# Counts from a piece's landing, a smaller memset, the last block in two halves, and packing dealt by a table

## The chip, the core and the metric

The kernel runs on one core of one Trainium2 chip. The metric is the device time of one execution, in microseconds; the kernel before takes 1273.65 us (median of three runs). The engines are TensorE (PE, with its weight loads as PEld), VectorE (DVE), ScalarE (ACT), GpSimd (POOL) and SyncE (SP), whose queue issues the large DMAs here.

## The reference

Two graph layers over one dense adjacency matrix of 8192 x 8192, with 64 features a node:

```
x:   (8192, 64) float32        adj: (8192, 8192) float32 of zeros and ones
# layer 0
deg = clip(sum(adj, axis=1) + 1, 1)
z   = concat([x, (adj @ x + x) / deg]) @ W0 + b
y   = layernorm(x + l2_normalize(relu(z)))
# layer 1, two hops
u = y
for k in range(2):
    u = tanh(concat([adj @ u, u], axis=1) @ W1[k])
out = layernorm(y + u)
```

`adj` has 268 MB, so it is read once. The kernel checks that it holds only zeros and ones, packs it to bits in SBUF while the first product runs, and makes the two products of layer 1 from the packed bits.

## The kernel before

**Streaming stage.** `adj` is cut into 8 x 8 blocks of 1024 x 1024. For each block row J the columns come in the order `ORDERS[J]`, each in two pieces, so that a block row has 16 steps and the stage 128 (step n = 16 J + s; the piece of step n is piece n). A piece is 2 MB and comes in two loads of 1 MB (128 x 2048 float32), each in one of four input slots `raw[:, u]`, with u = 0, 1 for even and 2, 3 for odd pieces. A piece passes through these hands:

1. SP issues its loads when the slots are free (L416 to L419).
2. VectorE *marks* each slot: 64 where the value is one, as bytes in `marks` (L905).
3. ScalarE *counts* the nonzero values of each slot in two instructions (L467); after the second, the slot is free (`counted`).
4. TensorE *packs*: 32 small matmuls of `marks` with powers of two (L648), into the PSUM bank `ps_pack`. There is one such bank, so a pack waits for the save of the one before (`pack_saved`).
5. VectorE *saves* the pack as bytes in `packed` (L910), and *expands* it into `planes` by eight operations (L923).
6. TensorE multiplies: 16 matmuls (a light step), or 24 where a column lies in a finished block row (a heavy step), since the first hop of layer 1 is then done as well (L657).

The orders are written out by hand. On TensorE, step n is: pack piece n + 1, multiply piece n, and in the first eight steps of a block weigh one tile of the block row before (L686). On VectorE, step n is: mark the first slot of piece n + 2, drain a weighed tile (L965 to L969), save piece n + 1, expand it, mark the second slot of piece n + 2, and in steps 8 to 14 of a block do parts of the row's norms (`FINISH`, L984 to L1008). Two of these parts need an inverse root from GpSimd (L580 and L582, L587 and L589). `save_acc` on ScalarE (L478) copies the sums of a block out of PSUM between two counts.

At the start GpSimd sets a third of the feature table to zero (L591, 128 x 8192 bfloat16), of which block row 0 reads only the first eight tiles.

**Second stage.** `UNITS` lists 150 units of half a block. Of each, VectorE takes two bits at a time from `packed` (`two_bits`, L1100 or, for both halves, L1115), ScalarE and VectorE widen them to `wide` (L503, L1129), and TensorE multiplies (L826). At the end of a row its sums are copied (L530), weighed with the row's own features (`weigh_own`, L786 and L788), and finished: addition, tanh on ScalarE, addition of `x1_sum` (made on GpSimd, L608), mean, square, variance, root on GpSimd, product, store. The last row does this in two halves after the last unit, with the seven operations of `finish_last` for both halves in turn.

## Time and profile before

| | |
|---|---|
| runs | 1273.53, 1273.65, 1277.28 us |
| profiled execution | 1273.58 us, span 1271.7 us |
| PE busy | 1195.5 us, 94% |
| DVE busy | 988.7 us, 78% |
| ACT busy | 899.5 us, 71% |
| POOL busy | 96.8 us, 8% |
| DMA | 274.64 MB; in the first 60% of the span 309 to 385 GB/s in a slice of a fortieth |

The span is the time from the first to the last instruction of the profiled execution, and the execution's own time is 1.9 us longer. Matmuls overlap by their modelled ends, so that PE's busy time says less than what stands ahead of a wait: where PE is idle, the profile names who ended the wait. The first 780 us or so are the streaming stage and the rest is the second stage.

### The profile page before, as it was taken

What the parts mean: (1) busy time and instruction counts of PE and PEld (TensorE: products, weight loads), DVE (VectorE), ACT (ScalarE), POOL (GpSimd) and SP (SyncE); (2) the same over time, 40 slices, a digit from 0 to 9 for tenths busy, and PEclk for the clock granted to TensorE, in tenths of its full rate; (3) what the DMA queues carried; (4) which work ended last, traced back from release to release, by engine and by line L of the source; (5) the groups of instructions that cost most, each with busy time, mean ns of one, the idle gap of its engine ahead of it and who ended that gap; (6) DMA issues with size and microseconds to landing.
All of it is one profiled execution on the core that took longest, in us unless ns stands there. A gap on an engine that the chain in (4) does not pass through costs nothing.

```text
span 1271.7 us, 25078 instructions
## 1 busy us (share of the span) xinstructions
PE 1195.5 (94%) x9510; PEld 819.7 (64%) x9510; DVE 988.7 (78%) x2641; ACT 899.5 (71%) x1310; POOL 96.8 (8%) x81
## 2 busy tenths in 40 slices
PE   3889989989999999999999999899999999999996
PEld 2445645645655655655655556778888888887775
DVE  7888898798898797798698687876655454778895
ACT  5778878778778678678668565675555555888783
POOL 3000020020020020010020011100000000010211
PEclk9899999999999999999999999899999999999998
DMA  9999999999999999899899880000000000000000
GB/s 322 381 385 370 372 377 364 366 381 356 364 374 375 343 350 379 319 355 361 309 359 346 322 323 4 1 1 1 1 1 1 1 1 1 1 9 9 18 17 19
DMA packets 88042, 274.64 MB, mean 216 GB/s; under 512 B 22384, under 2 KB 22384, under 8 KB 87920
## 3 DMA queue, kind: packets, MB, share of 16 engines
q1 hardware_dynamic: 86880, 272.73, 58.3%
q8 instruction: 79, 1.29, 0.4%
q10 hardware_dynamic: 1040, 0.26, 0.1%
q14 instruction: 43, 0.35, 0.1%
HBM read 270.88 MB, written 2.10 MB: 215 GB/s over the span
## 4 chain that ended last, share of the span: by engine, by line
PE 68%; DVE 15%; DMA 7%; POOL 4%; ACT 3%; issue 3%; DVEq 0%; POOLq 0%; ACTq 0%
PE acc L657 27%; PE acc L826 25%; DMA raw<-in_adj 7%; PE ps_pack L648 6%; DVE marks L905 6%; PE ps_epi L686 3%; ACT raw L467 3%; DVE planes L923 2%; PE ps_pack L788 2%; PE ps_pack L786 2%; POOL root L589 2%; DVE packed L910 1%; POOL root L582 1%; PE ps_epi L766 1%; PE ps_epi L801 1%
## 5 line engine op out<-in xcount | busy, mean ns | idle before, releaser
L467 ACT ACTIVATE raw<-raw 128x1024 f32<-128x1024 uint32 x512 | 535.8, 1048 | 193.2 <-DVE marks L905 192.0
L657 PE MATMUL acc<-planes,feats 128*128 128x512 fp8e4 x2512 | 569.1, 382 | 7.8 <-issue 7.8
L657 PEld LDWEIGHTS acc<-planes,feats 128*128 128x128 bf16 x2512 | 238.7, 98 | 279.6 <-issue 16.6
L905 DVE TENSOR_SCALAR marks<-raw 128x2048 uint8<-128x2048 f32 x256 | 314.4, 1241 | 26.2 <-DMA raw<-in_adj 25.8
L503 ACT ACTIVATE wide<-twos 128x2048 fp32r<-128x2048 fp8e4 x114 | 215.8, 1917 | 111.1 <-PE acc L826 100.8
L1129 DVE TENSOR_SCALAR wide<-twos 128x2048 fp32r<-128x2048 uint8 x114 | 139.4, 1223 | 74.8 <-PE acc L826 74.1
L648 PE MATMUL ps_pack<-pow,marks 128*128 128x64 bf16 x4096 | 141.8, 194 | 44.8 <-DVE marks L905 44.7
L648 PEld LDWEIGHTS ps_pack<-pow,marks 128*128 128x128 fp8e4 x4096 | 135.8, 98 | 67.7 <-issue 58.8
L923 DVE TENSOR_SCALAR planes<-packed 128x128 uint32<-128x128 uint32 x1024 | 150.9, 220 | 23.3 <-DVE packed L910 22.9
L826 PE MATMUL acc<-wide,x_high 128*128 128x512 f32 x512 | 126.7, 394 | 2.5 <-DVE wide L1129 2.2
L910 DVE TENSOR_SCALAR_CACHE_REDUCE packed<-ps_pack 128x512 uint8<-128x512 f32 x128 | 88.0, 687 | 36.8 <-PE ps_pack L648 36.6
L826 PEld LDWEIGHTS acc<-wide,x_high 128*128 128x128 f32 x512 | 96.3, 190 | 25.2 <-DVE wide L1129 4.4
L826 PE MATMUL acc<-wide,y_high 128*128 128x512 f32 x416 | 106.2, 400 | 0.5 <-DVE y_high L1165 0.5
L467 ACT ACTIVATION_READ_ACCUMULATOR raw<-raw 128x1 f32 x512 | 96.3, 188 | 0.0
L826 PEld LDWEIGHTS acc<-wide,y_high 128*128 128x128 f32 x416 | 78.5, 192 | 17.0 <-issue 1.2
L503 ACT ACTIVATE wide<-agg 128x2048 fp32r<-128x2048 fp8e4 x36 | 68.2, 1911 | 20.3 <-PE acc L826 16.3
L1100 DVE TENSOR_SCALAR twos<-packed 128x128 uint32<-128x128 uint32 x312 | 50.1, 224 | 39.0 <-ACT wide L503 37.2
L826 PE MATMUL acc<-wide,x_low 128*128 128x512 f32 x256 | 61.7, 394 | 3.3 <-DVE wide L1129 3.3
L826 PE MATMUL acc<-wide,x_mid 128*128 128x512 f32 x256 | 62.6, 393 | 0.0
L826 PEld LDWEIGHTS acc<-wide,x_low 128*128 128x128 f32 x256 | 47.1, 188 | 15.3 <-DVE wide L1129 5.9
L580 POOL TENSOR_SCALAR stat<-stat 128x8 f32<-128x8 f32 (+1 forms) x9 | 8.7, 969 | 630.7 <-DVE stat L987 630.7
L826 PEld LDWEIGHTS acc<-wide,x_mid 128*128 128x128 f32 x256 | 47.3, 188 | 9.4
(151 smaller groups left out, 960.5 us busy)
## 6 DMA issues: line engine op xcount, KB each, us to landing
raw<-in_adj SPq DMA_DIRECT2D x256, 1024.0 KB, 6.2
zpart<-in_x SPq DMA_DIRECT2D x7, 256.0 KB, 7.7
out<-result SPq DMA_DIRECT2D x7, 256.0 KB, 2.6
zpart<-in_x ACTq DMA_DIRECT2D x1, 256.0 KB, 9.2
out<-result SPq DMA_DIRECT2D x2, 128.0 KB, 2.0
w_own<-in_L_gnn_W SPq DMA_DIRECT2D x8, 16.0 KB, 6.5
w_a<-in_L_gnn_W SPq DMA_DIRECT2D x4, 16.0 KB, 6.6
w_y<-in_L_gnn_W SPq DMA_DIRECT2D x2, 16.0 KB, 6.7
```

The costliest lines, as they stand in the source:

```text
L467: ins = act.activation(words, words.bitcast(U32), ACT.Sign, accum_out=nonzero[:, tile:tile + 1, I])
L503: act.activation(out_ap, twos_of(u).bitcast(F8), ACT.Abs).then_inc(low_ready, 1)
L589: pool.tensor_tensor(root[:, cols], stat[:, cols], minus_half[:, cols], ALU.pow).then_inc(root_ready, 1)
L648: mm = pe.matmul(ps_pack[:, a * NW:(a + 1) * NW], marks[:, h, q, a * P:(a + 1) * P], pow2[:, q, :], start=q == 0, stop=q == QH - 1)
L657: mm = pe.matmul(acc[g][:, h, :], feats[g][:, I * TB + a, :], planes[:, h, a, :], start=(start or g in opens) and a == 0, stop=a == TB - 1 ...
L686: mm = pe.matmul(bank[:, at:at + weights.shape[1]], sums, weights, start=n == 0, stop=n == len(products) - 1, skip_group_check=True)
L826: mm = pe.matmul(acc[acc_of(key)][:, h, :], pair[:, a, :], wide[:, u % AHEAD, a, :], start=begins and a == 0, stop=a == TB - 1, skip_group ...
L905: dve.tensor_scalar(out_ap.bitcast(U8), raw[:, u, :], 1.0, 64.0, ALU.is_equal, ALU.mult).then_inc(marked, 1)
L910: dve.tensor_scalar(bytes_of(J, I, s % 2), ps_pack[:, :], 1.0, None, ALU.mult, ALU.add, accum_out=packsum[:, bass.ds((J * NB + I) * 2 + s ...
L923: ins = dve.tensor_scalar(wide[:, :, bit * NW // 4:(bit + 1) * NW // 4], words, shift, 0x40404040, op, ALU.bitwise_and)
L1100: ins = dve.tensor_scalar(room[:, :, g * NW // 4:(g + 1) * NW // 4], words, 6 - 2 * g, 0xC0C0C0C0, ALU.logical_shift_left, ALU.bitwise_and)
L1129: dve.tensor_scalar(out_ap, twos_of(u), 128.0, 2.0, ALU.is_ge, ALU.mult).then_inc(high_ready, 1)
```

## The change

- **Counts.** ScalarE waits for the landing of a slot and no longer for its mark, and writes its by-product into the free `twos` buffer instead of over the slot. SP waits for count and mark of a slot. `kept_y` moves from `twos` to `agg[0]`, and `save_acc` waits for its readers.
- **Memset.** GpSimd's memset of 8192 columns goes. VectorE sets the 1024 columns that are read, ahead of its first mark.
- **Packing.** `packing_order()` deals the packs to the steps, up to two in a step and up to three pieces ahead. Evaluated, it gives one pack (piece n + 1) to each step up to 22; two to the steps 23, 36, 39, 47 and 53; none to 25, 41, 46, 125, 126 and 127; and one to every other. From step 53 on TensorE packs piece n + 3 in step n.
- **Last block.** The last row's units are ordered by half, so that half 0 closes at unit 145 and half 1 at unit 149. Half 0 is weighed after unit 147, and `finish_last` for half 0 is spread over VectorE's turns from unit 149 on; the last eight units are taken from `packed` one by one.

```diff
-        for col in list(range(1, row + 1)) + [0]:
-            units += halves(row, col, 0, 1)
+        cols = list(range(1, row + 1)) + [0]
+        if row == LAST_ROWS[-1]:
+            units += [(row, col, h, 0, 1) for h in range(2) for col in cols]
+        else:
+            for col in cols:
+                units += halves(row, col, 0, 1)
...
+LOOKAHEAD = 3
+def packing_order():
+    packs, taken, pe, landed, packed_at = [], 0, 0.0, [0.0] * ALL, [0.0] * ALL
+    for n in range(ALL):
+        J, s = divmod(n, STEPS)
+        here = []
+        while taken + 1 < ALL and taken + 1 <= n + LOOKAHEAD and len(here) < 2:
+            p = taken + 1
+            landed[p] = max(landed[p - 1] + STREAM, packed_at[p - 2] + FREED if p > 1 else 0.0)
+            if p > n + 1 and landed[p] + MARKED > pe:
+                break
+            pe = max(pe, landed[p] + MARKED) + PACK
+            packed_at[p] = pe
+            here.append(p)
+            taken = p
+        packs.append(here)
+        heavy = ORDERS[J][s // 2] < J
+        pe += (HEAVY if heavy else LIGHT) + (WEIGH if J > 0 and s < TB else 0.0)
+    return packs
+STREAM, FREED, MARKED, PACK, LIGHT, HEAVY, WEIGH = 5.5, 3.0, 3.0, 1.1, 3.6, 5.3, 1.5
...
-        kept_y = twos[:, 0].rearrange("p a n -> p (a n)").bitcast(F32)
-        sq = agg[0][:, 0:TB * D]
+        signs = twos[:, :, :, :].rearrange("p h a n -> p h (a n)")
+        sq = kept_y = agg[0][:, 0:TB * D]
...
                             sp.wait_ge(counted, 4 * (J * NB + k) + (u - 3))
+                            sp.wait_ge(marked, 4 * (J * NB + k) + (u - 3))
...
-                    act.wait_ge(marked, J * 4 * NB + (4 * k + u + 1))
+                    act.wait_ge(raw_landed[u], J * (16 * NB) + 16 * (k + 1))
+                    slot = 4 * (J * NB + k) + u
+                    if slot > 1:
+                        act.wait_ge(counted, slot - 1)
...
-                        ins = act.activation(words, words.bitcast(U32), ACT.Sign,
+                        ins = act.activation(signs[:, u % 2, q * BLK:(q + 1) * BLK], words.bitcast(U32), ACT.Sign,
...
-            pool.memset(feats[YHI // P][:, :, :], 0.0).then_inc(consts, 1)
...
-                    if J * STEPS + s < ALL - 1:
-                        pack(J, s + 1)
+                    for p in PACKS[J * STEPS + s]:
+                        pack(p // STEPS, p % STEPS)
...
+                    if k == 2 * NB - 1 and LAST_HALF + 2 == u:
+                        weigh_own(k, [0])
...
+                    packs = PACKS[n]
+                    if packs:
+                        mark_next(packs[0], 0)
                     if J > 0 and 1 <= s <= TB:
                         drain(J - 1, s - 1, 1, USES_1 * (J - 1) + 1 + s)
+                    if packs:
+                        save_pack(packs[0])
                     if n + 1 < ALL:
                         dve.wait_ge(pack_saved, n + 2)
+                        nxt = (n + 1) // STEPS
+                        expand(nxt, ORDERS[nxt][(s + 1) % STEPS // 2], (s + 1) % 2, n if n > 0 else None)
+                    if packs:
+                        mark_next(packs[0], 1)
+                    for p in packs[1:]:
+                        mark_next(p, 0)
+                        save_pack(p)
+                        mark_next(p, 1)
...
+            dve.memset(feats[YHI // P][:, 0:TB, :], 0.0).then_inc(lo_zeroed, 1)
...
+                if 0 <= u - FIRST_LAST < 7:
+                    finish_last(u - FIRST_LAST, 0)
             for n in range(7):
-                for half in range(2):
-                    finish_last(n, half)
+                if n > NU + 9 - FIRST_LAST:
+                    finish_last(n, 0)
+                finish_last(n, 1)
```

TensorE at steps 35 to 37 (block 2), in the program before. `ps_pack` rows are packs, `acc` rows the products, `ps_epi` rows the weighing:

```order
L648 MATMUL ps_pack<-pow,marks 128x64 x32
L657 MATMUL acc<-planes,feats 128x512 x16
L686 MATMUL ps_epi<-w_own,featT 128x128
L686 MATMUL ps_epi<-w_y,agg 128x64
L686 MATMUL ps_epi<-w_a,agg 128x64
L686 MATMUL ps_epi<-w_a,agg 128x128
L648 MATMUL ps_pack<-pow,marks 128x64 x32
L657 MATMUL acc<-planes,feats 128x512 x24
```

The same place in the changed program:

```order
L696 MATMUL ps_pack<-pow,marks 128x64 x32
L705 MATMUL acc<-planes,feats 128x512 x16
L734 MATMUL ps_epi<-w_own,featT 128x128
L734 MATMUL ps_epi<-w_y,agg 128x64
L734 MATMUL ps_epi<-w_a,agg 128x64
L734 MATMUL ps_epi<-w_a,agg 128x128
L696 MATMUL ps_pack<-pow,marks 128x64 x64
L705 MATMUL acc<-planes,feats 128x512 x24
```

Two packs of 32 matmuls stand in a row ahead of the products of step 36. VectorE in step 36 before, from the marks ahead of its drain (the second slot of piece 37 and the first of piece 38) on:

```order
L905 TENSOR_SCALAR marks<-raw 128x2048 x2
L965 SCALAR_TENSOR_TENSOR z<-ps_epi,rdeg,bias 128x64
L967 COPY zpart<-ps_epi 128x64
L969 TENSOR_TENSOR z<-z,ps_epi 128x64
L910 TENSOR_SCALAR packed,packsum<-ps_pack 128x512
L923 TENSOR_SCALAR planes<-packed 128x8x16 x8
L905 TENSOR_SCALAR marks<-raw 128x2048 x2
```

And in the changed program:

```order
L955 TENSOR_SCALAR marks<-raw 128x2048 x2
L1023 SCALAR_TENSOR_TENSOR z<-ps_epi,rdeg,bias 128x64
L1025 COPY zpart<-ps_epi 128x64
L1027 TENSOR_TENSOR z<-z,ps_epi 128x64
L968 TENSOR_SCALAR packed,packsum<-ps_pack 128x512
L981 TENSOR_SCALAR planes<-packed 128x8x16 x8
L955 TENSOR_SCALAR marks<-raw 128x2048 x2
L968 TENSOR_SCALAR packed,packsum<-ps_pack 128x512
L955 TENSOR_SCALAR marks<-raw 128x2048 x2
```

A second save with two more marks follows; the second slot of piece 38 is still marked after the expansion, as before. The end of the program on VectorE, from the variance of row 14 (L1244) on, before:

```order
L1244 TENSOR_REDUCE stat<-nonzero 128x8
L1247 TENSOR_TENSOR result<-result,root 128x512
L1264 TENSOR_TENSOR result<-ps_pack,zpart 128x256
L1264 TENSOR_TENSOR result<-ps_epi,zpart 128x256
L1268 TENSOR_TENSOR result<-result,src 128x256 x2
L1271 TENSOR_REDUCE mean<-result 128x4 x2
L1274 SCALAR_TENSOR_TENSOR result<-mean,result 128x256 x2
L1278 TENSOR_TENSOR nonzero<-result 128x256 x2
L1281 TENSOR_REDUCE stat<-nonzero 128x4 x2
L1284 TENSOR_TENSOR result<-result,root 128x256 x2
```

And after (the addition of half 0, L1334, stands two rows ahead of it):

```order
L1334 TENSOR_TENSOR result<-ps_pack,zpart 128x256
L1309 TENSOR_TENSOR nonzero<-result 128x512
L1311 TENSOR_REDUCE stat<-nonzero 128x8
L1338 TENSOR_TENSOR result<-result,src 128x256
L1314 TENSOR_TENSOR result<-result,root 128x512
L1341 TENSOR_REDUCE mean<-result 128x4
L1344 SCALAR_TENSOR_TENSOR result<-mean,result 128x256
L1348 TENSOR_TENSOR nonzero<-result 128x256
L1351 TENSOR_REDUCE stat<-nonzero 128x4
L1354 TENSOR_TENSOR result<-result,root 128x256
L1334 TENSOR_TENSOR result<-ps_epi,zpart 128x256
L1338 TENSOR_TENSOR result<-result,src 128x256
```

All seven operations of half 0 stand ahead of those of half 1, and its second one (L1338) ahead of row 14's last (L1314).

## Rows read from the trace of the kernel before

**Rows 1.** Stretches: blocks 0 to 3, and after the last unit; columns in its head.

```profile
core 0: us, PE busy (x) PEld busy (x) DVE busy (x) ACT busy (x) POOL busy (x), PEclk, DMA share, GB/s
22.30:117.20 94.90, 82.81 (x792) 43.44 (x790) 81.54 (x224) 73.05 (x137) 0.00 (x0) 0.95 1.03 377
117.20:208.50 91.30, 82.86 (x858) 49.56 (x854) 78.57 (x233) 72.51 (x136) 8.20 (x4) 1.00 1.00 369
208.50:299.50 91.00, 85.61 (x875) 51.02 (x871) 78.96 (x233) 72.07 (x136) 8.20 (x4) 1.00 0.99 370
299.50:391.60 92.10, 88.84 (x891) 52.77 (x888) 78.86 (x233) 72.49 (x136) 8.20 (x4) 1.00 0.99 367
...
1256.80:1271.70 14.90, 3.75 (x34) 3.58 (x32) 6.53 (x15) 1.43 (x3) 4.62 (x6) 0.73 0.17 38
```

**Rows 2.** Costliest groups, busy and mean, then idle before; SP's waits.

```profile
L648 PE MATMUL ps_pack<-pow,marks 128*128 128x64 bf16 x4096 | 141.8, 194 | 44.8 <-DVE marks L905 44.7
L923 DVE TENSOR_SCALAR planes<-packed 128x128 uint32<-128x128 uint32 x1024 | 150.9, 220 | 23.3 <-DVE packed L910 22.9
SPq L418 <- ACT raw L467: 638.6, 251, 8.9
```

**Rows 3.** Timeline of the start: start, length, engine, line, instruction, idle before.

```profile
1.24 1.76 DVE L1065 MEMSET feats<- 128x2048 uint32 x1 [1.24 <-PEq L1412]
4.75 6.92 POOL L591 MEMSET feats<- 128x8192 bf16 x1
6.24 7.93 DVE L905 TENSOR_SCALAR marks<-raw 128x2048 uint8<-128x2048 f32 x2 [3.23 <-DMA raw<-in_adj]
12.97 1.06 ACT L467 ACTIVATE raw<-raw 128x1024 f32<-128x1024 uint32 x1 [10.44 <-DVE marks L905]
```

**Rows 4.** Stretches of 2.5 us at the start, columns as rows 1.

```profile
12.50:15.00 2.50, 0.69 (x14) 0.72 (x15) 2.47 (x4) 2.03 (x4) 0.58 (x1) 1.00 1.01 403
15.00:17.50 2.50, 1.17 (x22) 1.01 (x19) 2.40 (x9) 2.24 (x6) 0.00 (x0) 1.00 0.54 141
```

**Rows 5.** Timeline of TensorE, then VectorE, in step 36.

```profile
228.72 1.10 PE L648 MATMUL ps_pack<-pow,marks 128*128 128x64 bf16 x32
229.66 5.34 PE L657 MATMUL acc<-planes,feats 128*128 128x512 fp8e4 x24
...
230.16 0.68 DVE L910 TENSOR_SCALAR_CACHE_REDUCE packed<-ps_pack 128x512 uint8<-128x512 f32 x1
...
231.02 1.18 DVE L923 TENSOR_SCALAR planes<-packed 128x128 uint32<-128x128 uint32 x8 [0.18 <-DVE packed L910]
232.11 1.22 DVE L905 TENSOR_SCALAR marks<-raw 128x2048 uint8<-128x2048 f32 x1
```

**Rows 6.** Timeline of GpSimd's root and the packs in block 2's norms.

```profile
259.01 1.15 POOL L580 TENSOR_SCALAR stat<-stat 128x8 f32<-128x8 f32 x1 [70.00 <-DVE stat L987]
260.24 2.95 POOL L582 TENSOR_TENSOR root<-stat,minus_half 128x8 f32<-128x8 f32 x1
...
263.23 0.69 DVE L990 SCALAR_TENSOR_TENSOR z<-z,root 128x512 f32<-128x512 f32 x1
...
269.02 1.09 PE L648 MATMUL ps_pack<-pow,marks 128*128 128x64 bf16 x32 [1.18 <-DVE marks L905]
...
274.58 1.09 PE L648 MATMUL ps_pack<-pow,marks 128*128 128x64 bf16 x32 [1.01 <-DVE marks L905]
```

**Rows 7.** Timeline of the end, units and last two rows.

```profile
1253.25 3.79 PE L826 MATMUL acc<-wide,x_low 128*128 128x512 f32 x16
...
1255.05 0.69 DVE L1244 TENSOR_REDUCE stat<-nonzero 128x8 f32<-128x512 f32 x1
...
1256.10 1.65 POOL L589 TENSOR_TENSOR root<-stat,minus_half 128x8 f32<-128x8 f32 x1
...
1257.72 1.04 POOL L608 TENSOR_TENSOR src<-y_mid 128x512 f32<-128x512 f32 x1
...
1263.90 0.74 DVE L1281 TENSOR_REDUCE stat<-nonzero 128x4 f32<-128x256 f32 x2
...
1264.69 1.02 POOL L589 TENSOR_TENSOR root<-stat,minus_half 128x4 f32<-128x4 f32 x1
...
1267.35 0.42 DVE L1284 TENSOR_TENSOR result<-result,root 128x256 f32<-128x256 f32 x1 [1.18 <-POOL root L589]
```

More of the change, by code:

```diff
@@ L156 @@
 L2_EPS = 1e-12
+LOOKAHEAD = 3
[18 more added lines that the diff above has]
+STREAM, FREED, MARKED, PACK, LIGHT, HEAVY, WEIGH = 5.5, 3.0, 3.0, 1.1, 3.6, 5.3, 1.5
+PACKS = packing_order()
+TAKEN = [max(sum(PACKS[:n + 1], [0])) for n in range(ALL)]
 def gnn_kernel(nc, x, adj, w0, b0, w1, out):
@@ L375, in gnn_kernel @@
         BITS = 1 + 2 * QH
-        CONSTS = 4
+        CONSTS = 3
         WEIGHTS = 16 * 18
@@ L484, in save_own, with counts_before @@
                 act.activation(featT[:, :], ps_epi[:, :], ACT.Copy).then_inc(epi_drained, 1)
-            for J in range(NB):
-                for s in range(STEPS):
-                    count_step(J, s)
-                    if J > 0 and s < 2:
-                        save_acc(J - 1, s)
-                    if s == STEPS - 1:
+            def counts_before(n):
+                return min(TAKEN[n] + 1, ALL - 1)
+            for p in range(ALL):
+                count_step(p // STEPS, p % STEPS)
+                for J in range(NB):
+                    for h in range(2):
+                        if J < NB - 1 and counts_before((J + 1) * STEPS - 2 + h) == p:
+                            save_acc(J, h)
+                    if counts_before(J * STEPS + STEPS - 2) == p:
                         save_own(J)
@@ L551, in _ @@
                         take_tanh(k)
-            last = result[:, (2 * NB - 1) % 2]
-            for half in range(2):
-                act.wait_ge(own_read, 2 * NB + half)
-                ap = last[:, 4 * half * D:4 * (half + 1) * D]
-                act.activation(ap, ap, ACT.Tanh).then_inc(tanh_done, 1)
+            last_tanh(1)
             with act.If(unless_binary(act) > 0):
@@ L778, in weigh_own @@
                     pe.wait_ge(own_read, k)
-                for half in range(2):
+                for half in part:
                     pe.wait_ge(sums_saved, SAVED[(kind, ROWS[k]), half])
@@ L906, in mark, with mark_next, save_pack @@
                                   ALU.mult).then_inc(marked, 1)
-            def save_pack(J, s, I):
-                dve.wait_ge(pack_done, J * STEPS + (s + 1))
+            def mark_next(p, pair):
+                if p + 1 < ALL:
+                    mark((p + 1) // STEPS, (p + 1) % STEPS, pair)
+            def save_pack(p):
+                J, s = divmod(p, STEPS)
+                I = ORDERS[J][s // 2]
+                dve.wait_ge(pack_done, p + 1)
                 dve.tensor_scalar(bytes_of(J, I, s % 2), ps_pack[:, :], 1.0, None, ALU.mult, ALU.add,
@@ L1087, in two_bits @@
                 row, col, h = UNITS[u][:3]
-                if u >= THIRD:
+                if THIRD <= u and row != LAST_ROWS[-1] or THIRD <= u < LAST_UNITS and row == LAST_ROWS[-1]:
                     if h == 0:
@@ L1316, in _ @@
                             finish_row(k, 5)
-            dve.wait_ge(out_stored[LAST % 2], 16 * ((LAST - NB) // 2))
-            dve.wait_ge(upper_read, NB - 1 - ROWS[LAST])
+                if 0 <= u - FIRST_LAST < 7:
+                    finish_last(u - FIRST_LAST, 0)
             for n in range(7):
-                for half in range(2):
-                    finish_last(n, half)
+                if n > NU + 9 - FIRST_LAST:
+                    finish_last(n, 0)
+                finish_last(n, 1)
             with dve.If(unless_binary(dve) > 0):
```

40 lines of the change are left out of this document (24 added, 16 removed).

## The prediction

> **What bounds the kernel now.** I read the stretches by block first, then who waits for whom, then the timeline at the four places that the edits touch.
>
> The streaming stage is eight blocks of sixteen steps. In the stretches [rows 1] the first four blocks take 94.9, 91.3, 91.0 and 92.1 us. TensorE is idle in them for 12.1, 8.4, 5.4 and 3.3 us (length less busy PE), VectorE is busy for 79 to 82 us, and DMA moves 367 to 377 GB/s with a busy share of 0.99 to 1.03. Three resources are nearly full together, and DMA is the fullest: a step reads 2 x 1.048 MB, which at 370 GB/s is 5.67 us against a measured 5.7. The grouped rows [rows 2] name TensorE's idle time: 44.8 us before the packing matmuls (L648), nearly all ended by VectorE's marks (L905). SP's queue waits 638.6 us for ScalarE's counts, which release the input slots.
>
> TensorE's granted clock is 0.95 in block 0 and 1.00 in the three after it [rows 1]; I take no change of time from it. The profiled execution took 1273.58 us with a span of 1271.7 us, the median of the runs is 1273.65; my sum is made against 1273.6.
>
> **The smaller memset.** A mark takes 1.22 us [rows 5], but the two that start at 6.24 us take 7.93 us together, and ScalarE's first count starts at 12.97 us, released by the first of them. GpSimd's memset (L591) runs from 4.75 for 6.92 us [rows 3], so it ends at 11.67, and 11.67 + 1.22 = 12.89. The first mark stands still behind the memset, for some 5.4 us. The new memset on VectorE is a quarter of the one at 1.24 us that took 1.76 us, about 0.5 us, inside VectorE's 3.23 us of idle time before the first mark: free. If that cover were gone it would cost its 0.5 us.
>
> The Trainium skill, SBUF — State Buffer, § Who interferes with whom, says that VectorE in a two-port mode and GpSimd exclude each other for a whole instruction, whoever started first. By that rule, the trace agrees here: blocked to the memset's end, not slowed in proportion.
>
> Of the 5.4 us less than half arrives. DMA binds block 0, and it lost only what its own gap cost: from 15.0 to 17.5 us it moves 141 GB/s, against 403 in the stretch before [rows 4]. That is (403 - 141) / 403 x 2.5 = 1.6 us, and the refill, with two slots in flight instead of four, starts slowly behind it. **Start: -2.5 us** (bounds -1.6 and -5.4).
>
> **Counts from landing.** Count and mark now run side by side, and a slot comes free at the later of the two, instead of mark 1.2 us + two counts of 1.06 us [rows 3]: some 2.1 us sooner for each slot. Where DMA's queue is already full (share 1.03 and 0.99) this lengthens the queue and not the rate. Taken: 0, since the rows show no faster steady rate; the other end is in the rivals. The added wait on `marked` in SP costs nothing: behind it in SP's queue stand only the next loads, which wait for the same marks anyway.
>
> **The table.** Each of the steps 23, 36, 39, 47 and 53 packs two pieces; 25, 41, 46 and the last three pack none. What two in a row cost is read from step 36 in before [rows 5]. TensorE packs piece 37 from 228.72 and the products follow at 229.66. VectorE saves that pack at 230.16, expands piece 37 at 231.02 for 1.18 us, and then marks the second half of piece 38, 232.11 + 1.22 = 233.33. In before this runs under products of 5.34 us. In the new program, TensorE's second pack stands ahead of those products and VectorE's order is unchanged: save, expand, mark. So the second pack cannot start before 233.35, and TensorE stands idle from 229.7: **3.6 us for each double**. Nothing covers it, because the products are queued behind the pack on the same engine.
>
> Each double also moves one pack of 0.95 us forward (228.72 to 229.66), given back where none is packed.
>
> - Up to block 2: the first double lies in a block where pieces arrive barely in time. It costs 3.6 us, and the free step 25 returns some 2.6 of it, since VectorE and DMA are behind there (my choice between 0 and all of it). -2.5 + 1.0 = **-1.5 us**.
> - Doubles 36, 39, 53: 3 x (3.6 + 0.95) = 13.7. Double 47 lies in the last step of a block, without the drain that stands ahead of the save in the other three: 3.2 + 0.95 = 4.1. Together **+17.8 us**.
> - Step 41 without a pack. Steps 41 to 45 are bound by VectorE, which has marks, a save, an expansion and two operations of the norm to do: packs come 274.58 - 269.02 = 5.56 us apart, and each waits 1.0 us for the marks [rows 6]. Leaving out two marks and a save (2 x 1.22 + 0.68 [rows 5]) shortens VectorE's step by 3.1 us. But its next norm operation (L990, 263.23) needs GpSimd's root, whose two operations start at 259.01 and end at 260.24 + 2.95 = 263.19, 4.2 us in all, just as long as VectorE had marks to make [rows 6]. What the empty step frees is then spent waiting for the root. **+0.2 us** net, bounds -3 and +1.
> - Step 46 without a pack: heavy products (5.34 us) hide what VectorE saves; the pack and the wait before it go: 0.95 + 1.0 = **-2.0 us**.
> - From step 48 on, the wait of 0.18 us between save and expand (22.9 us over 128 steps [rows 2]) is gone, since the piece that is saved is no longer the one expanded. It counts only where VectorE binds, some three steps of a block: 5 x 3 x 0.18 = **-2.7 us**.
> - Last steps: two packs fewer, **-1.9 us**.
>
> Streaming stage: -1.5 + 17.8 + 0.2 - 2.0 - 2.7 - 1.9 = **+9.9 us**.
>
> The same rule of the Trainium skill (SBUF — State Buffer, § Who interferes with whom) would make GpSimd faster in step 41, where no mark of 1.2 us holds the pair: the root took 1.65 us in the tail [rows 7] and 2.95 us beside marks [rows 6]. The stage would then be 1 us shorter, +8.9 us. No row of the trace shows a root beside an empty step.
>
> **The last block in two halves.** The intent is that half 0 is finished under half 1's products. VectorE's order says otherwise. Half 0's seven operations stand ahead of all of half 1's, and its second one needs x1_sum, which GpSimd makes only after row 14's root. In before [rows 7]: reduction at 1255.05, root at 1256.10 for 1.65 us, x1_sum at 1257.72 for 1.04 us. In the new order that reduction comes after half 0's first addition, which waits for its weighing: the last two units start at 1253.25 in before, the weighing takes their place for half of 3.75 us [rows 1], and 1253.25 + 1.9 + 0.42 + 0.7 for the operation between is 1256.3, 1.2 us later. So x1_sum is ready at 1258.76 + 1.2 = 1259.95. Then, at 0.42 us an operation, 0.7 for a whole row, and GpSimd's root done 1.45 us after the reduction (1264.27 to 1265.71): addition 1260.4, row 14's product 1261.1, four operations 1262.8, root 1264.3, product 1264.7. Only now comes half 1: addition, tanh, addition 1.4 us, four operations 1.7, root 1.45, product 0.45: 1269.7. In before the last product ends at 1267.35 + 0.42 = 1267.77. **Tail: +2.0 us**, bounds -3.1 (half 0 out of the way: 0.9 of weighing, 1.0 of VectorE's shared steps, 1.2 of GpSimd's first root) and +3. The last eight units are unpacked one by one instead of in pairs, four more groups of four operations, 4 x 4 x 0.22 (the mean of L923 [rows 2]) = 3.5 us on VectorE over eight units of 1.9 us, of which it fills 1.22 each; no cost taken, and 1 us if a unit waits for it.
>
> **Sum.** 1273.6 + 9.9 + 2.0 = 1285.5 us.
>
> **The rivals.**
> A, faster: DMA has more in it. 403 GB/s stands in [rows 4]; with slots freed 2.1 us sooner, pieces come faster, and the stock of packed ones fills TensorE's idle time of blocks 1 to 3. Three quarters of 8.4 + 5.4 + 3.3 us is -12.8; start -2.5, doubles 47 and 53 in heavy steps +6.8, tail +2.0: 1267.1 us. Against it: a queue full at 1.03 still moves only 377 GB/s. The Trainium skill, HBM Reference, § Specifications (TRN2), states about 425 GB/s for a core that streams alone; by it a piece would take 4.9 us and DMA would bind no block, which is this rival. No block's row shows more than 377.
> B, no change: the doubles stall as I say, but VectorE runs ahead during each stall, and the steps that it binds afterwards (5.4 us in block 2, 3.3 in block 3) lose their idle time. 9.9 - 8.7 + 2.0: 1276.8 us. Against it: the root.
> C, slower still: being two pieces further ahead takes 2 x 5.67 = 11.3 us more of a full queue by step 53. Where marks of the second piece wait for a landing, half of that comes on top: 1291.1 us. It decides if VectorE's marks wait over 5 us longer for DMA than before.
> That the doubles are none (the second piece marked in time) is excluded by VectorE's order; what is left of it is in A.
>
> **Chances.** Forecast 0.53, A 0.17, B 0.18, C 0.12. A measurement here can tell 0.3%, 3.8 us, from no change. Faster is A, 0.17; same is B, 0.18; slower is the forecast and C, 0.65. The forecast's own range is 1281 to 1290 us. The range that should hold 8 in 10 is 1268 to 1292 us: it takes in B and the near half of A, and C beyond its price.
>
> **What would show it.** In the changed profile: the first mark in 1.2 us; the wait of L648's successor for marks up by some 14 us, the five longest after the start about 3.5 us; VectorE's idle time before L990's successor for GpSimd's root grown in blocks 1 and 2; the eight blocks' stretch ending some 10 us later; half 1's addition after half 0's product in the tail. I am wrong if the block lengths 2 and 3 do not grow, if DMA's rate in blocks 1 to 3 exceeds 385 GB/s, or if the tail after the last unit is under 14 us.

## The result, and the profile after

| | before | after |
|---|---|---|
| median of four runs | 1273.59 us | 1290.62 us |
| range | 1271.69 to 1277.28 | 1290.53 to 1293.98 |
| profiled execution, span | 1271.7 us | 1288.7 us |
| mean granted clock | 0.989 | 0.982 |

The ratio is 1.0136, 95% interval 1.0116 to 1.0155: slower, 5 us beyond the 1285.5 us that were predicted. It lies 0.6 us over the forecast's own range of 1281 to 1290 us and inside the one of 1268 to 1292 us. By stages: from the first instruction to the last product of the streaming stage 782.7 us became 797.2 (+14.5, predicted +9.9), and the rest went from 489.1 to 491.5 us (+2.5, predicted +2.0).

The stretches of blocks 0 to 3 and of the end in the profile after, to be held against [rows 1]:

```profile
19.00:115.30 96.30, 80.54 (x793) 42.54 (x791) 81.99 (x225) 72.09 (x134) 0.00 (x0) 0.98 1.03 379
115.30:206.80 91.50, 83.66 (x857) 50.43 (x853) 78.65 (x233) 72.72 (x136) 6.12 (x4) 0.98 0.97 369
206.80:313.90 107.10, 92.54 (x908) 54.86 (x905) 81.34 (x237) 77.07 (x144) 5.86 (x4) 0.94 0.90 340
313.90:410.60 96.70, 92.30 (x923) 55.10 (x919) 80.82 (x237) 77.12 (x144) 8.06 (x4) 0.96 0.96 364
1273.80:1288.70 14.90, 2.23 (x18) 1.86 (x16) 5.92 (x14) 1.01 (x2) 3.87 (x6) 0.68 0.17 38
```

Blocks 2 and 3, which hold the doubles 36, 39, 47 and 53, took 16.1 and 4.6 us more. DMA did not speed up there. It fell to 340 GB/s, and the granted clock fell from 1.00 to 0.94 and 0.96, in stretches in which TensorE is busy for over 85% of the time.

The grouped rows of after (L696 packs, L955 marks, L968 saves, L981 expands, L519 is `save_acc`), against [rows 2]:

```profile
L955 DVE TENSOR_SCALAR marks<-raw 128x2048 uint8<-128x2048 f32 x256 | 308.4, 1219 | 32.1 <-DMA raw<-in_adj 31.9
L981 DVE TENSOR_SCALAR planes<-packed 128x128 uint32<-128x128 uint32 x1024 | 150.1, 220 | 11.7 <-DVE packed L968 6.2 <-PE acc L705 5.4
L696 PE MATMUL ps_pack<-pow,marks 128*128 128x64 bf16 x4096 | 144.6, 195 | 50.3 <-DVE marks L955 50.3
L519 ACT ACTIVATE agg<-acc 128x512 f32<-128x512 f32 x48 | 25.2, 598 | 49.6 <-PE acc L705 49.6
```

TensorE waits 50.3 us for marks (44.7 before), 5.6 us more where the prediction looked for some 14. The sum alone hides the change: the start gave 3 us back, other steps 8.5, and five new waits of 3.1 to 3.9 us, 17.1 us together, came in. The wait between save and expand fell from 22.9 to 6.2 us. ScalarE waits 49.6 us before `save_acc`, where it waited 5.4 before. That is not the table's doing: with the counts alone it already waits 46.0 us, as shown below.

**The table, as the chip ran it.** TensorE, VectorE and ScalarE at the double of step 47:

```profile
290.32 1.22 DVE L955 TENSOR_SCALAR marks<-raw 128x2048 uint8<-128x2048 f32 x1
291.46 0.42 DVE L1090 CAST feats<-agg 128x512 bf16<-128x512 f32 x1
291.91 0.69 DVE L1092 TENSOR_TENSOR feats<-agg,feats 128x512 bf16<-128x512 f32 x1
292.52 1.17 DVE L981 TENSOR_SCALAR planes<-packed 128x128 uint32<-128x128 uint32 x8
292.70 7.03 PE L705 MATMUL acc<-planes,feats 128*128 128x512 fp8e4 x24 [2.40 <-DVE feats L1092]
293.61 1.22 DVE L955 TENSOR_SCALAR marks<-raw 128x2048 uint8<-128x2048 f32 x1
299.57 1.10 PE L696 MATMUL ps_pack<-pow,marks 128*128 128x64 bf16 x32
299.77 1.57 ACT L519 ACTIVATE agg<-acc 128x512 f32<-128x512 f32 x3 [11.40 <-PE acc L705]
300.70 0.69 DVE L968 TENSOR_SCALAR_CACHE_REDUCE packed<-ps_pack 128x512 uint8<-128x512 f32 x1 [5.88 <-PE ps_pack L696]
...
301.58 1.18 DVE L981 TENSOR_SCALAR planes<-packed 128x128 uint32<-128x128 uint32 x8 [0.18 <-DVE packed L968]
...
302.67 2.35 DVE L955 TENSOR_SCALAR marks<-raw 128x2048 uint8<-128x2048 f32 x2
...
304.04 1.87 PE L696 MATMUL ps_pack<-pow,marks 128*128 128x64 bf16 x32 [3.37 <-DVE marks L955]
...
305.71 7.40 PE L705 MATMUL acc<-planes,feats 128*128 128x512 fp8e4 x24
```

The order is the predicted one: pack, save, expand, mark, and only then the second pack, 3.37 us after the end of the first. Two things were not foreseen. The pack after the pause takes 1.87 us instead of 1.10, and the products 7.40 us instead of 5.34. And step 46, which packs nothing, starts its products no earlier, since they wait 2.40 us for VectorE's `feats` (L1092, the features of the finished row).

**The end.** The timeline of after, against [rows 7]:

```profile
1270.47 0.42 DVE L1334 TENSOR_TENSOR result<-ps_pack,zpart 128x256 f32<-128x256 f32 x1 [0.98 <-PE ps_pack L836]
...
1272.59 1.65 POOL L638 TENSOR_TENSOR root<-stat,minus_half 128x8 f32<-128x8 f32 x1
...
1274.20 1.04 POOL L656 TENSOR_TENSOR src<-y_mid 128x512 f32<-128x512 f32 x1
...
1275.28 0.42 DVE L1338 TENSOR_TENSOR result<-result,src 128x256 f32<-128x256 f32 x1 [3.06 <-POOL src L656]
...
1276.43 0.39 PE L836 MATMUL ps_epi<-w_x_pair,agg 128*128 128x64 f32 x2
...
1279.43 0.43 DVE L1354 TENSOR_TENSOR result<-result,root 128x256 f32<-128x256 f32 x1 [1.42 <-POOL root L638]
1279.77 0.42 DVE L1334 TENSOR_TENSOR result<-ps_epi,zpart 128x256 f32<-128x256 f32 x1
```

Half 0 waits 3.06 us for `x1_sum`, and half 1, whose weighing ends at 1276.82, is added at 1279.77, behind half 0's root and product.

### The profile page after: what moved, and what is told of

Read it like the earlier page. It is cut to its first block, busy times and chain, and to the rows that moved or that the text cites. A ratio compares the mean times of both kernels' runs of the same rounds, so it can differ in the third digit from the quotient of the medians.

```text
span 1288.7 us, 25605 instructions
## 1 busy us (share of the span) xinstructions
PE 1202.3 (93%) x9510; PEld 824.1 (64%) x9510; DVE 977.8 (76%) x2658; ACT 903.2 (70%) x1310; POOL 82.9 (6%) x80
## 4 chain that ended last, share of the span: by engine, by line
PE 72%; DVE 9%; DMA 8%; issue 4%; ACT 3%; POOL 2%; SPq 0%; DVEq 0%; POOLq 0%; ACTq 0%
PE acc L705 31%; PE acc L874 25%; DMA raw<-in_adj 8%; PE ps_pack L696 7%; PE ps_epi L734 3%; DVE marks L955 3%; ACT twos L506 2%; PE ps_pack L836 2%; PE ps_pack L834 2%; DVE planes L981 2%; POOL root L638 1%; PE ps_epi L814 1%; PE ps_epi L849 1%; DVE packed L968 1%; DVE wide L1196 1%
## 5 line engine op out<-in xcount | busy, mean ns | idle before, releaser
L506 ACT ACTIVATE twos<-raw 128x1024 uint8<-128x1024 uint32 x512 | 536.1, 1052 | 145.9 <-DMA raw<-in_adj 145.9
L705 PE MATMUL acc<-planes,feats 128*128 128x512 fp8e4 x2512 | 573.2, 384 | 10.2 <-issue 7.8
L955 DVE TENSOR_SCALAR marks<-raw 128x2048 uint8<-128x2048 f32 x256 | 308.4, 1219 | 32.1 <-DMA raw<-in_adj 31.9
L696 PE MATMUL ps_pack<-pow,marks 128*128 128x64 bf16 x4096 | 144.6, 195 | 50.3 <-DVE marks L955 50.3
L696 PEld LDWEIGHTS ps_pack<-pow,marks 128*128 128x128 fp8e4 x4096 | 139.0, 99 | 70.8 <-issue 61.6
L981 DVE TENSOR_SCALAR planes<-packed 128x128 uint32<-128x128 uint32 x1024 | 150.1, 220 | 11.7 <-DVE packed L968 6.2
L968 DVE TENSOR_SCALAR_CACHE_REDUCE packed<-ps_pack 128x512 uint8<-128x512 f32 x128 | 88.0, 688 | 53.6 <-PE ps_pack L696 53.3
L506 ACT ACTIVATION_READ_ACCUMULATOR twos<-raw 128x1 f32 x512 | 97.7, 191 | 0.0
L874 PEld LDWEIGHTS acc<-wide,y_high 128*128 128x128 f32 x416 | 78.9, 193 | 17.4 <-issue 1.5
L519 ACT ACTIVATE agg<-acc 128x512 f32<-128x512 f32 x48 | 25.2, 598 | 49.6 <-PE acc L705 49.6
L874 PEld LDWEIGHTS acc<-wide,x_low 128*128 128x128 f32 x256 | 47.1, 188 | 15.3 <-DVE wide L1196 5.9
L1023 DVE SCALAR_TENSOR_TENSOR z<-ps_epi,rdeg,bias 128x64 f32<-128x64 f32 x60 | 16.7, 282 | 48.6 <-PE ps_epi L734 48.5
```

Of the source, the lines that this page charges most:

```text
L506: ins = act.activation(signs[:, u % 2, q * BLK:(q + 1) * BLK], words.bitcast(U32), ACT.Sign, accum_out=nonzero[:, tile:tile + 1, I])
L696: mm = pe.matmul(ps_pack[:, a * NW:(a + 1) * NW], marks[:, h, q, a * P:(a + 1) * P], pow2[:, q, :], start=q == 0, stop=q == QH - 1)
L705: mm = pe.matmul(acc[g][:, h, :], feats[g][:, I * TB + a, :], planes[:, h, a, :], start=(start or g in opens) and a == 0, stop=a == TB - 1 ...
L874: mm = pe.matmul(acc[acc_of(key)][:, h, :], pair[:, a, :], wide[:, u % AHEAD, a, :], start=begins and a == 0, stop=a == TB - 1, skip_group ...
L955: dve.tensor_scalar(out_ap.bitcast(U8), raw[:, u, :], 1.0, 64.0, ALU.is_equal, ALU.mult).then_inc(marked, 1)
L968: dve.tensor_scalar(bytes_of(J, I, s % 2), ps_pack[:, :], 1.0, None, ALU.mult, ALU.add, accum_out=packsum[:, bass.ds((J * NB + I) * 2 + s ...
```

## The experiments

Twelve kernels ran. Times are medians; "before" stands for its runs beside them (1275.0 to 1275.7 us). The ratio to before carries the comparison. "Step n starts" is the start of its first product (L657 in before) in the trace of the kernel. Kernels with the same first steps differ by up to 1.7 us at step 16, so differences between two kernels below that say nothing there; differences from step to step within a block repeat to some 0.1 us.

### Which parts cost and which give

**one_ahead** is after without its table:

```diff
-PACKS = packing_order()
+PACKS = [[n + 1] if n + 1 < ALL else [] for n in range(ALL)]
```

> The changed kernel with one pack per step again (piece n + 1 in step n, none in the last), all else as changed. Theory (the doubled packs hold TensorE still, and its clock falls behind the pauses): the 14.5 us of the streaming stage go, and the stage ends about 3 us earlier than in the kernel before; with the 2.5 us that the second stage and the end keep, 1272.5 to 1274.5 us. Rival (counts from landing, or ScalarE's reordered copies, cost the time in blocks 2 and 3): the stage stays longer than before, 1280 us or more.

Measured: 1269.3 us, 0.9954 [0.9934, 0.9975]. The table costs 21 us, and the rest is a gain, larger than either theory had.

**memset_alone** is before with the smaller memset (the diff's lines on `feats[YHI // P]`, `consts` and `lo_zeroed`).

> The kernel before with only the smaller memset on VectorE. Theory: the first mark takes 1.2 us instead of 6.7, DMA's gap at 15 us closes in part, and the stage ends 1.5 to 3 us earlier: 1270.5 to 1272 us. Rival (DMA binds block 0 and the gap comes from the counts behind the marks, so that the start is hidden): 1273.5 us, no change.

Measured: 1272.2 us, 0.9974 [0.9960, 0.9988]. Step 0 starts 3.2 us earlier and step 16 1.9 us.

**counts_alone** is before with the diff's lines on `counted`, `marked`, `signs` and `kept_y`.

> The kernel before with only the counts from a slot's landing. Theory (DMA's queue is full, freeing slots sooner only lengthens it): block 1 and 2 lose under 1 us, the wait of ScalarE in block 3 (0.8 us) goes, 1272 to 1274 us. Rival (DMA has more in it once it is fed sooner): blocks 1 to 3 shorter by 3 us each, 1266 us or less, with DMA over 380 GB/s in them.

Measured: 1267.3 us, 0.9937 [0.9914, 0.9960]. Step 0 starts as before, step 8 2.2 us earlier, step 28 5.7 and step 51 6.5. This is the gain that I had put at 0. It lies in blocks 0 and 1 for the most part, and not in each of the first blocks as the rival had it. The block 1 stretch of this kernel, then its marks (L911) and its `save_acc` (L484):

```profile
117.00:208.50 91.50, 86.03 (x902) 52.22 (x901) 82.32 (x243) 76.37 (x142) 8.21 (x4) 1.00 0.99 381
```

```profile
L911 DVE TENSOR_SCALAR marks<-raw 128x2048 uint8<-128x2048 f32 x256 | 313.9, 1244 | 13.6 <-DMA raw<-in_adj 13.2
L484 ACT ACTIVATE agg<-acc 128x512 f32<-128x512 f32 x48 | 25.2, 597 | 46.0 <-PE acc L663 42.1 <-DVE y_high L1022 3.8
```

DMA moved 381 GB/s where it moved 369, at the same busy share of 0.99 and 1.00, and the marks' wait for data halved (25.8 before). That wait is no measure of the gain, though: in counts_memset, which is next, it is 23.2 us for the same gain. ScalarE, no longer held by the marks, now comes early to `save_acc` at each block's end and waits there for the last product.

**counts_memset** has both, and is after without table and halves.

> The kernel before with the counts from landing and the smaller memset: the changed kernel without its table and without the last block in two halves. Theory: the gains add up to 3 us or slightly more, 1269.5 to 1271.5 us, and the difference from the run with the halves (one pack per step) is the price of the halves, 2 to 3 us. Rival (the halves gain 3 us at the end as intended): this run is slower than that one.

Measured: 1266.7 us, 0.9925 [0.9898, 0.9952]. The memset adds nothing to the counts by the end of the stage (-6.6 us against -6.7). one_ahead, which has the halves as well, takes 2.6 us more by the medians, their price as expected.

**late_slots** asks whether the counts give their 6.7 us because slots come free sooner. It is counts_alone with a later release:

```diff
-sp.wait_ge(counted, 4 * (J * NB + k) + (u - 3))
+sp.wait_ge(counted, 4 * (J * NB + k) + (u - 3) + 1)
```

> The kernel before with the counts from landing alone (1267.3 us, 0.9937 of before), with one edit: SyncE issues a load into a slot of raw only when the count of the next slot is done as well, which is about 2.5 us later, where the kernel before issued it. If the 6.7 us that these counts gave come from the slots that are free 2.2 us earlier, and so from loads that start and land earlier, they go with this edit: 1273 to 1277 us, and the marks wait for the data as long as in the kernel before (25 us or more). Rival: they come from ScalarE and VectorE, whose order no longer ties each count to a mark: 1266 to 1269 us, with marks that wait about 13 us for the data.

Measured: 1287.2 us, 1.0096 [1.0062, 1.0131], in runs spread from 1277 to 1301 us. The gain is gone and more with it. The same two rows of this kernel:

```profile
117.00:208.50 91.50, 83.48 (x858) 49.80 (x856) 79.09 (x234) 73.62 (x137) 8.19 (x4) 1.00 0.96 370
```

```profile
L911 DVE TENSOR_SCALAR marks<-raw 128x2048 uint8<-128x2048 f32 x256 | 315.7, 1241 | 52.7 <-DMA raw<-in_adj 49.9 <-PE ps_pack L654 2.4
```

The rival (it is ScalarE's and VectorE's order) falls, since that order is the same here. The edit overshot, and the time is 10 us above my expectation: the starts stay within 2.5 us of before up to step 40, where counts_alone is 5.7 us ahead, and most of the rest is lost just behind block edges (steps 50, 66, 98 and 114), where ScalarE's `save_acc` stands ahead of a count that the release now needs. That it is this order was not tried by itself. So the run shows that the gain hangs on the release of the slots; it does not measure its size.

### What a double costs, and what a lead gives

The base is counts_memset. A table of its own deals the packs:

```diff
+def dealt(doubles, skips):
+    packs, taken = [], 0
+    for n in range(ALL):
+        count = 2 if n in doubles else 0 if n in skips else 1
+        here = list(range(taken + 1, min(taken + count, ALL - 1) + 1))
...
+PACKS = dealt((36,), ())
```

**double36**: step 36 packs two, and packing stays one piece further ahead.

> The base is the kernel with the counts from landing and the smaller memset alone (1266.7 us, 0.9925 of before): no halves, one piece packed in each step. The one change: step 36 packs two pieces, and from there on packing stays one piece further ahead. Prediction's theory: TensorE stands for the second piece's marks, which VectorE does only behind the save and the expansion: the products of step 36 come 3.6 us later, and with the clock that falls after the pause about 4.2 to 6; little of it comes back, so 1270.5 to 1272.5 us. Rival: the further lead lets more be moved or saves later waits, and the whole comes back by the end of the streaming stage: 1266.5 to 1267.5.

Measured: 1268.7 us, 0.9942 [0.9920, 0.9963].

**double36_free41**: `dealt((36,), (41,))`.

> As the kernel with step 36 doubled, and step 41 packs nothing, so that the lead is given back there. If the pack that is left out comes off TensorE's path, step 41's products come 2.4 to 3.4 us earlier than with the double alone, and the sum is 1268 to 1269 us. By the prediction's step (GpSimd's root ends last there, and eats the pack that is gone) nothing comes back: 1270.5 to 1272.5.

Measured: 1272.7 us, 0.9982 [0.9967, 0.9997].

**double36_free46**: `dealt((36,), (46,))`.

> As the kernel with step 36 doubled, and step 46 packs nothing. The prediction had 2.0 us come back there: 1268.5 to 1270.5. The trace of the changed kernel says that step 46's products wait for a part of x1 that VectorE writes later than they could start, so that nothing comes back: within 0.5 us of the kernel with the double alone, and the step's products start no earlier.

Measured: 1273.1 us, 0.9987 [0.9974, 1.0001].

The starts of steps, in us behind the same steps of counts_memset (after in the last column):

```
step   double36   free41   free46    after
 35     +0.13     -0.16    +0.26     +3.86
 36     +5.84     +5.44    +5.57     +9.60
 37     +7.32     +7.27    +6.18    +10.15
 41     +7.24     +6.25    +6.10    +13.34
 43     +6.51     +4.92    +5.38    +11.74
 46     +5.72     +4.91    +4.58    +10.94
 54     +5.79     +4.91    +4.58    +26.77
 70     +4.58     +4.89    +4.56    +25.56
110     +2.01     +4.86    +4.52    +22.98
127     +1.08     +4.86    +4.52    +21.11
```

One double costs 6 to 7.4 us. A lead that is kept gives it back bit by bit: 5.3 us from step 37 to step 110, in the steps of every block in which VectorE's work is the longest, and 0.9 us in step 126, which has nothing left to pack. So for double36 the price was over the first theory's 4.2 to 6 us, and the rival had the return. A lead that is given up in step 41 returns 2.4 us by step 43 and nothing after; one given up in step 46 returns 1.6 us before it, in the same steps as double36, and nothing in step 46 itself, as the trace of after had said. That double36_free46 would stay within 0.5 us of double36 was wrong: it is 4.4 us slower, 3.4 of them in the stage, since the lead that it gave up earns nothing in the steps behind. double36_free41 falls where the prediction's step put it, but by another way: 2.4 us did come back, and nothing after.

**marked_first** is the whole of after, with another order on VectorE in the five doubles:

```diff
+if len(packs) > 1:
+    mark_next(packs[0], 1)
 if packs:
     save_pack(packs[0])
 ...
-if packs:
+if len(packs) == 1:
     mark_next(packs[0], 1)
```

> The whole changed kernel with one edit: in the five steps with two packs VectorE writes the second marks of the second piece ahead of the first piece's save, and not behind save and expansion. If the stall is that order on VectorE, the second pack waits for the save alone: 1.2 to 2.1 us in place of 3.6 to 4 at each of the five, no clock falls (7 us), and the time is 1271 to 1277 us in place of 1290.6. Rival: the second piece's marks wait for the data of the piece, which land no earlier, so the pause stays as long: 1287 to 1291 us, and the moved marks wait for the transfer.

Measured: 1281.6 us, 1.0047 [1.0029, 1.0065]: between the two theories. 9 of the 21 us went, by the median and by the start of step 127. The table below has the five doubles, each with TensorE's pause between the two packs, the landing of the second piece and the end of its marks:

```
step   after: pause   marked_first: pause   landing   marks end   second pack
 23       3.62              2.83            154.53     155.78       156.49
 36       3.90              2.92            229.60     230.85       231.56
 39       3.11              1.49            250.58     254.41       255.12
 47       3.37              0.84            289.88     294.29       298.15
 53       3.10              1.95            337.17     338.42       339.13
```

In steps 39 and 47 the piece lies ready and the order was the price. In steps 23 and 36 (and in part 53) the marks now start 0.03 us after the landing: the piece is not there sooner, and the rival is right for these. ScalarE shows what else this order brings, here at step 47:

```profile
293.07 1.22 DVE L955 TENSOR_SCALAR marks<-raw 128x2048 uint8<-128x2048 f32 x1
...
296.21 1.10 PE L696 MATMUL ps_pack<-pow,marks 128*128 128x64 bf16 x32
296.41 1.57 ACT L519 ACTIVATE agg<-acc 128x512 f32<-128x512 f32 x3 [9.35 <-PE acc L705]
...
298.15 1.09 PE L696 MATMUL ps_pack<-pow,marks 128*128 128x64 bf16 x32 [0.84 <-issue]
...
298.34 1.08 ACT L506 ACTIVATE twos<-raw 128x1024 uint8<-128x1024 uint32 x1
```

`save_acc` waits 9.35 us for the block's last product, where it waits 5.2 us in counts_memset at the same block's end. The count behind it starts at 298.34, of a slot whose mark had ended at 293.16, and is done at 300.45. So the slot is released 7 us behind its mark, and the steps 49 to 52 lose 3.7 us more, which I put down to late landings.

**The clock** in stretches of after behind its pauses in step 47 (3.37 us) and, last, step 53 (3.10 us):

```profile
305.70:313.10 7.40, 7.40 (x34) 3.02 (x32) 3.07 (x4) 4.41 (x10) 0.00 (x0) 0.72 0.98 368
313.10:319.00 5.90, 5.90 (x84) 4.08 (x81) 4.78 (x16) 5.85 (x12) 0.00 (x0) 1.00 0.77 272
346.90:354.20 7.30, 7.30 (x31) 3.14 (x29) 2.97 (x4) 5.79 (x12) 0.00 (x0) 0.73 1.02 407
```

The same products of step 47 in marked_first, behind a pause of 0.84 us:

```profile
299.10:304.40 5.30, 5.30 (x34) 2.47 (x31) 3.18 (x7) 5.30 (x11) 0.00 (x0) 1.00 0.53 175
```

Behind the pauses of after the clock was granted at 0.72 and 0.73 on the mean, between its levels of 1.2 and 2.4 GHz (0.5 and 1.0), and a step of 5.34 us took 7.3 to 7.4. The pack behind the pause ran at 0.50 in steps 36, 47 and 53 and took 1.87 us instead of 1.10. In steps 23 and 36 of marked_first, behind 2.83 and 2.92 us, the products took 5.25 us instead of 3.62 and 6.99 instead of 5.34. Behind pauses of 0.84, 1.49 and 1.95 us they kept their length. So they did behind 3.11 us in step 39 of after, and behind 2.4 us in step 46 of marked_first and double36_free46, though not in after's own: the fall is likely behind a long pause, not certain. The Trainium skill, TensorE: Matmul & The Clock Gate, § HAM oscillation, describes waits between groups of matmuls after which each group starts at the low clock. The trace agrees for the steps above, and not for every pause: 3.11 us in step 39 lowered nothing.

### A version from what was found

**lead39**: the base with one double, in step 39, where the piece lies ready, with the marks first (`dealt((39,), ())` and the edit of marked_first).

> The base is again the kernel with the counts from landing and the smaller memset alone (1266.7 us, 0.9925 of before). Step 39 packs two pieces, VectorE writes the second marks of the second piece ahead of the first save there, and the piece of lead is kept to the end. The trace of the kernel with step 36 doubled shows two things: a standing lead gave 6.2 us back between steps 39 and 127 (+7.32 fell to +1.08), and at step 36 part of the pause was the second piece's landing; at step 39 the piece has landed before the pack. If both hold, the double costs 2.6 us here (as in the kernel with the marks first) and 6.2 come back: 1262 to 1264 us. Rival: the pause is the same wherever the double stands, since the save and the pack between the two pieces are the price: 1266 to 1268.

Measured: 1263.3 us, 0.9912 [0.9889, 0.9935], as the first theory had it. Step 39 in its trace (L697 packs, L954 marks, L967 saves, L706 multiplies):

```profile
244.03 1.10 PE L697 MATMUL ps_pack<-pow,marks 128*128 128x64 bf16 x32
...
244.69 1.22 DVE L954 TENSOR_SCALAR marks<-raw 128x2048 uint8<-128x2048 f32 x1
...
245.83 0.68 DVE L967 TENSOR_SCALAR_CACHE_REDUCE packed<-ps_pack 128x512 uint8<-128x512 f32 x1
...
246.62 1.09 PE L697 MATMUL ps_pack<-pow,marks 128*128 128x64 bf16 x32 [1.49 <-DVE packed L967]
...
247.55 3.62 PE L706 MATMUL acc<-planes,feats 128*128 128x512 fp8e4 x16
```

In the stretch behind it the clock is granted in full:

```profile
246.60:252.00 5.40, 5.38 (x60) 3.59 (x61) 5.08 (x13) 4.22 (x8) 0.00 (x0) 1.00 1.03 419
```

The step's start moves by 2.6 us against step 38's, and step 127 has gained 6.3 us on counts_memset's since step 40, of which 0.9 us is the pack that is left out near the end. The net gain over counts_memset is 3.7 us in the stage by these steps, and 0.9912 against 0.9925 in the runs, whose intervals overlap: that it beats before is shown, that it beats counts_memset only by its trace. Its span, 1260.3 us, also holds 2.4 us of a faster start of the second stage that I can't put down to the edit.

**lead39_72**: a second double in step 72.

> As the kernel with step 39 doubled, and step 72 doubled too, so that packing is two pieces ahead from there on. If what a lead gives is TensorE's idle time in the steps in which VectorE's own work is the longest (three quarters of a us each, in six to eight steps from 74 to 110), the second lead pays about its price of 2.5 us: within 1.5 us of the other kernel. Rival: with two pieces ahead the four slots of raw are too few, transfers start later and the marks wait for them: 3 us or more slower than with the one lead.

Measured: 1265.9 us, 0.9935 [0.9914, 0.9957]. Against lead39's steps, step 71 starts 0.2 us later, step 72 2.8 and step 127 1.5: the second double costs 2.6 us and 1.3 come back, 0.9 of them by one pack fewer at the end. It doesn't pay its price. In the stage the 1.5 us are what the first theory allowed; the medians lie 2.6 us apart, with intervals that overlap. The slots suffice: the marks wait 28.7 us for data against 25.1.

### The halves

**halves_turns** is one_ahead with the finish of the last row in turns, as in before:

```diff
-if 0 <= u - FIRST_LAST < 7:
-    finish_last(u - FIRST_LAST, 0)
 for n in range(7):
-    if n > NU + 9 - FIRST_LAST:
-        finish_last(n, 0)
-    finish_last(n, 1)
+    for half in range(2):
+        finish_last(n, half)
```

> The changed kernel with one piece packed in each step (1269.3 us, 0.9954 of before) and one edit more: the last block's units stay in two halves, but VectorE does the last row's operations in turns of the halves after the loop, as before. By the prediction's step half 1's addition stands behind half 0's operations and its root in VectorE's order, and in turns that wait goes: 1266.5 to 1268 us. Rival: what the halves cost is in the units themselves, whose expansion is issued in halves, and the turns return nothing or lose the head start: 1269 to 1271.5.

Measured: 1270.6 us, 0.9963 [0.9949, 0.9978], against 0.9954 for one_ahead: no difference. From the stage's end to the end of the span one_ahead takes 491.3 us, halves_turns 491.4, counts_memset 488.9. The difference lies ahead of the last unit's last product; behind it the three take 14.5, 14.8 and 14.7 us. The end of halves_turns (L576 copies half 1's sums, L587 is tanh):

```profile
1251.81 1.52 DVE L1314 TENSOR_TENSOR result<-result,root 128x512 f32<-128x512 f32 x1 [2.05 <-POOL root L638]
1253.26 0.41 DVE L1334 TENSOR_TENSOR result<-ps_pack,zpart 128x256 f32<-128x256 f32 x1
...
1253.70 0.42 ACT L587 ACTIVATE result<-result 128x256 f32<-128x256 f32 x1 [5.15 <-DVE result L1334]
1254.02 0.58 ACT L576 ACTIVATE agg<-acc 128x512 f32<-128x512 f32 x1
...
1254.75 0.41 PE L834 MATMUL ps_epi<-w_own,featT 128*128 128x64 f32 x2 [1.86 <-ACT agg L576]
```

In turns, half 0's addition waits behind row 14's root on VectorE, its tanh waits for it on ScalarE, and the copy of half 1's sums, which the last product released at 1252.9, stands behind that tanh. One order holds half 1 on VectorE, the other on ScalarE.

## Why the prediction came out as it did

The direction, the mechanism and the place were right: the doubles of blocks 2 and 3 stall TensorE for VectorE's marks. The sum was 5 us short, and errors of both signs lie beneath it, so that it came this near is in part luck. After's starts against counts_memset's, and counts_memset's against before's, give each term:

| term | predicted | measured |
|---|---|---|
| memset and counts | -2.5 and 0 | -6.6 |
| double 23 with free 25 | +1.0 | +3.8 |
| doubles 36, 39, 53 | +13.7 | +17.4 |
| free 41 | +0.2 | -3.4 |
| free 46 and double 47 | -2.0 + 4.1 | +9.0 |
| small gains of the lead | -2.7 | -3.8 |
| last steps | -1.9 | -1.9 |
| stage | +9.9 | +14.5 |
| rest | +2.0 | +2.5 |

- **Memset.** The first mark takes 1.23 us and starts at 6.16, as said, and alone the edit gives some 2 us. Together with the counts it gives nothing more by the stage's end.
- **"Taken: 0" for the counts** is a step that failed by its reading. A busy share of 1.03 with 377 GB/s was read as a full machine. It was not: a share of 0.99 carried 381 GB/s over block 1 with slots freed sooner, and before itself has the rate in a short stretch of block 2:

```profile
214.60:220.00 5.40, 5.40 (x59) 3.50 (x57) 5.22 (x18) 4.05 (x9) 0.00 (x0) 1.00 1.03 420
```

  The rival A had this right in kind. It put start and slots at 15.3 us together, and they gave 6.6.
- **The doubles.** The pause of 3.6 us holds: 3.62, 3.90, 3.11, 3.37 and 3.10 measured. So does the reason: in all five the second piece had landed before VectorE came to it. But at 23 and 36 it had landed only 1.0 us before (153.62 and 154.63, 229.61 and 230.64), so that with the marks first the pause there shrinks by no more than 0.8 and 1.0 us.
- **"I take no change of time from it"**, said of the clock, missed the largest term. The products of steps 23, 36, 46, 47 and 53 take 7.3 us more than in before (1.1, 0.6, 1.7, 2.1 and 1.9), and the packs behind the pauses of steps 23, 36, 47 and 53 2.9 us more, at granted clocks of 0.50 to 0.91. Without these 10.2 us the terms would sum to 4.3 us, below the 9.9.
- **Free step 41: "what the empty step frees is then spent waiting for the root".** It was not: 3.4 us came back by step 46. Of these 1.6 also come back in double36, which packs in step 41, so the free step's own part is 1.8 us. VectorE waits 1.15 us for the root, whose two operations end 2.11 us after the first of them starts:

```profile
267.52 0.36 POOL L629 TENSOR_SCALAR stat<-stat 128x8 f32<-128x8 f32 x1 [80.22 <-DVE stat L1045]
267.96 1.67 POOL L631 TENSOR_TENSOR root<-stat,minus_half 128x8 f32<-128x8 f32 x1
269.67 0.69 DVE L1048 SCALAR_TENSOR_TENSOR z<-z,root 128x512 f32<-128x512 f32 x1 [1.15 <-POOL root L631]
```

  In before they took 4.18 us beside marks [rows 6]. The rule of the Trainium skill (SBUF — State Buffer, § Who interferes with whom) that the prediction set beside its term, and did not follow, is the one that the trace bears out: without marks beside it, GpSimd's root is as fast as in the tail.
- **Free step 46: -2.0** gave nothing, since its products wait for VectorE's `feats`. I read the wait before the pack and not the one behind it.
- **The rival B** (VectorE runs ahead and returns 8.7 us in blocks 2 and 3) has its mechanism in the trace as well: of the distance to counts_memset 3.4 us go in steps 41 to 46, in part by the free step, and 1.1 in steps 58 and 62.
- **The rival C** has its number, 1291.1 us, and its sign: the marks' wait for DMA grew by 6.1 us (25.8 to 31.9), over its point of 5. But its mechanism isn't in TensorE's time. In the five doubles the second piece had landed 1.0 to 10.7 us before its marks began, and from block 1 on after falls further behind counts_memset only in the doubles, in the step behind each, and in step 46. Pauses (17.1 us), packs moved forward (4.8) and the clock (10.2) make up 32.1 of the 32.7 us that the steps of the doubles and step 46 lose. That the time meets C's price is chance.
- **The tail** went as laid out: half 1's addition behind half 0's product, 3.0 us after its weighing was done, and the last units' products later by the 1.7 us of half 0's weighing ahead of them. The explanation is only half shown: in turns the time is the same, for another wait.

## What to carry to other kernels

A buffer that is released earlier can speed up a DMA queue whose busy share already reads 1.0. The share didn't tell: the best rate in a short stretch of the old kernel, 420 GB/s, would have been the better sign. Work that is pulled ahead costs least where its input lies ready and the engine before it has already been told to prepare it. One such lead, taken where it is cheap and kept, did better (1263.3 us) than five of which three were given back (1281.6 with the same order of marks, and with the 2.6 us of the halves). And put a price on every new pause of TensorE that includes slower matmuls behind it.

## What the runs showed of the hardware that was not expected

- The granted clock falls behind single pauses of about 3 us in a stretch in which TensorE is otherwise busy: 0.72 and 0.73 over the next 7.3 us, so that the pauses of 3.37 and 3.10 us in steps 47 and 53 cost 2.8 and 2.7 us on top, pack and products together. Behind pauses up to 1.95 us no product was longer. The drop differs from kernel to kernel for one place: step 36 took 5.89, 6.83, 7.18, 5.95 and 6.99 us in five kernels.
- The DMA engines' busy share says little about their rate. Over blocks 0 to 3 of before it was 0.99 to 1.03 at 367 to 377 GB/s, over block 2 of lead39 1.00 at 389, and in two stretches of 5.4 us of before 1.05 at 359 and 1.03 at 420.
